# Two PSUM evacuations ahead of a low part at the quarter boundary, and the next block's normalisation ahead of the high parts on ScalarE

## The reference

```python
x = x + tanh(g_xattn) * attention(layernorm(x), ctx)    # 32 query heads, 8 key heads, dim 128
x = x + tanh(g_ffn) * ffn(layernorm(x))

def ffn(x):                                             # x is 2048 x 1024
    routing = softmax(x @ gate_w.T)                     # 8 experts
    in_scale  = routing @ in_channel_scale
    out_scale = routing @ out_channel_scale
    return (x * in_scale) @ sign(weight).T * out_scale + bias
```

## Time and profile before

| | |
|---|---|
| median of 3 runs | 1588.42 us |
| the profiled execution, its own time | 1589.38 us |
| its span, first to last instruction | 1587.6 us |
| TensorE busy (share of the span) | 1494.5 us (94%) |
| VectorE | 1034.2 us (65%) |
| GpSimd | 722.6 us (46%) |
| ScalarE | 615.2 us (39%) |
| mean granted TensorE clock, of full speed | 0.976 |

### The profile page before, as it was taken

The page is one execution under the profiler, slowest core; times in us unless marked ns, Lnnn a source line. Parts: engine busy times, 40 slices in busy tenths (PEclk is TensorE's granted clock), DMA queues, the critical chain, the costliest instruction groups (busy, mean ns, idle before and its releaser), DMA issues. The chain is left out here.

```text
span 1587.6 us, 26175 instructions
## 1 busy us (share of the span) xinstructions
PE 1494.5 (94%) x8720; PEld 1312.1 (83%) x8720; DVE 1034.2 (65%) x2375; ACT 615.2 (39%) x1183; POOL 722.6 (46%) x586
## 2 busy tenths in 40 slices
PE   6899999999999999999999399999999999769998
PEld 6778888888888888888888299999999999747776
DVE  6737878887788878887788545545545545555552
ACT  5722222322222222222222255555555555344442
POOL 6735454555546455455554333333333333135543
PEclk9999999999999999999999699999999999869999
DMA  7731122221322212222122794246954234332211
GB/s 275 270 100 54 41 79 75 73 66 40 86 66 73 66 42 83 66 73 66 53 66 66 227 398 151 74 126 202 389 189 126 79 115 124 100 146 85 95 71 62
DMA packets 90991, 184.02 MB, mean 116 GB/s; under 512 B 8976, under 2 KB 34064, under 8 KB 90768
## 3 DMA queue, kind: packets, MB, share of 16 engines
q1 hardware_dynamic: 86848, 178.95, 35.2%
q10 hardware_dynamic: 4080, 4.26, 0.8%
HBM read 129.70 MB, written 53.48 MB: 115 GB/s over the span
## 5 line engine op out<-in xcount | busy, mean ns | idle before, releaser
L51 PE MATMUL q_ps<-x_hi,w_hi 128*128 128x512 f32 x1024 | 399.5, 390 | 3.4 <-PEq L66 3.4
L53 PE MATMUL q_ps<-x_hi,w_lo 128*128 128x512 f32 x1024 | 400.9, 391 | 0.0
L52 PE MATMUL q_ps<-x_lo,w_hi 128*128 128x512 f32 x1024 | 400.0, 391 | 0.0
L913 DVE TENSOR_TENSOR vw_lo<-vw_ps,vw_hi 64x256 fp32r<-64x256 f32 x512 | 216.2, 422 | 241.0 <-ACT vw_hi L873 235.8
L902 POOL TENSOR_TENSOR w_lo<-w_raw,w_hi 128x512 fp32r<-128x512 f32 x128 | 166.1, 1299 | 297.3 <-ACT w_hi L865 297.3
L838 PE MATMUL acc_ps<-vw_hi,x_hi 128*128 128x256 f32 x1024 | 291.4, 285 | 4.9 <-DVE ahead_y L930 4.0
L839 PE MATMUL acc_ps<-vw_lo,x_hi 128*128 128x256 f32 x1024 | 290.6, 284 | 0.0
L840 PE MATMUL acc_ps<-vw_hi,x_lo 128*128 128x256 f32 x1024 | 290.5, 284 | 0.0
L873 ACT CAST vw_hi<-vw_ps 64x256 fp32r<-64x256 f32 x512 | 188.2, 368 | 177.7 <-PE vw_ps L53 172.9
L595 POOL TENSOR_TENSOR q_lo<-rot,q_hi 128x512 fp32r<-128x512 f32 x128 | 165.2, 1296 | 190.6 <-ACT q_hi L561 190.5
L51 PEld LDWEIGHTS q_ps<-x_hi,w_hi 128*128 128x128 f32 x1024 | 192.7, 188 | 45.0 <-issue 3.6
(11 more groups left out here) (132 smaller groups left out, 2448.3 us busy)
## 6 DMA issues: line engine op xcount, KB each, us to landing
w_raw<-in_wo SPq DMA_DIRECT2D x128, 256.0 KB, 2.8
w_raw<-in_wq SPq DMA_DIRECT2D x32, 512.0 KB, 5.2
probs_scratch<-pt_hi SPq DMA_DIRECT2D x64, 256.0 KB, 2.6
probs_scratch<-pt_lo SPq DMA_DIRECT2D x64, 256.0 KB, 3.2
x_hi<-probs_scratch SPq DMA_DIRECT2D x32, 512.0 KB, 8.0
x_lo<-probs_scratch SPq DMA_DIRECT2D x32, 512.0 KB, 9.6
x_in<-in_x SPq DMA_DIRECT2D x16, 512.0 KB, 4.7
ahead_y<-in_x SPq DMA_DIRECT2D x8, 1024.0 KB, 6.3
```

Of the source, the lines that this page charges most:

```text
L51: pe.matmul(out, hi, rhs_hi, start=first, stop=False, **kw)
L52: pe.matmul(out, hi, rhs_lo, start=False, stop=False, **kw)
L53: return pe.matmul(out, lo, rhs_hi, start=False, stop=last, **kw)
L913: done = nc.vector.tensor_tensor(vw_lo[at], vw_ps[i][b * SK:(b + 1) * SK, h, :], vw_hi[at].bitcast(F32), ALU.subtract)
```

## The change

Three things are done.

1. In `project`, VectorE makes the low part of the next quarter's head pair 0 as before, then evacuates banks 0 and 1, then makes the low part of head pair 1, then evacuates banks 2 and 3.
2. In `feed`, ScalarE normalises block i+1 right after the copy of the transposed routing and before the four high parts of block i.
3. GpSimd waits, once, before slot 1, for all stores of `x_q` to memory.

```diff
@@ project, VectorE, quarter @@
                 if following is not None:
-                    for hp in range(VW_AHEAD):
-                        values_low(*following, hp)
+                    values_low(*following, 0)
                 dve.wait_ge(x_q_in, 16 * (pair * NQ + q + 1))
                 for bank in range(NACC):
+                    if following is not None and bank == NACC // 2:
+                        values_low(*following, 1)
                     if bank < NACC - 1:
@@ feed, ScalarE, slot @@
                     nc.scalar.copy(r_stack_t[0:R, j, :], r_ps[0:R, 0:BT]).then_inc(r_stack_t_ready, 1)
+                if has(i, -1):
+                    normalise(i + 1, 1 - j)
+                if has(i, 0):
                     wait(act, f_done, NC * (i - 1))
                     high(i, j, 0)
                     high(i, j, 1)
@@ @@
                     high(i, j, 3)
                 some_signs(i, 7, KT)
-                if has(i, -1):
-                    normalise(i + 1, 1 - j)
                 some_signs(i + 1, 0, 3)
@@ feed, GpSimd @@
             slot(0, 0)
+            pool.wait_ge(x1_stored, 16 * B // PB * NQ)
             slot(1, 1)
```

## The result

The changed kernel took 1572.73 us, the median of 4 runs (1570.04 to 1574.38), against 1588.23 for the kernel before: ratio 0.9898, 95% interval [0.9881, 0.9915]. Measured two more times it took 1570.3 and 1570.81 us against 1588.21 and 1588.61: [0.9871, 0.9905] and [0.9875, 0.9913]. It is 15.5 to 17.9 us faster; 1571.4 was forecast. The profiled execution after has a span of 1571.5 us.

What follows compares the result with a forecast made beforehand. TensorE, busy 94% of the span, was taken as the bound. Terms -5.3 - 7.9 - 3.8 = -17.0 us took the profiled 1589.38 to 1572.4, and 0.96 lower for the median: 1571.4 us; 8-in-10 range 1568.5 to 1575.5.

Steps and rivals of the forecast that it cites:

- The three waits that the sum names: TensorE's waits: evacuation at quarter boundaries and `x1n` in steady slots gone; block 1's from 9.3 to about 5.5 us.
- Quarter boundary: `project`: 7 boundaries of 0.80 us won, 5.6 us, less 0.3 for a possible hold: -5.3 us.
- the 0.3 us for a hold at bank 2: Quarter boundary in `project`: allowance for bank 2's matmul waiting on its evacuation; bounds nothing to 1.0 us in all.
- Rival 1: Quarter boundaries: bank 2 is held after all, 3 to 5.6 us lost, 1574 to 1577 us; chance 0.09.
- Steady slots: `feed`: six waits of transposes for the normalised block go, 1.32 us each: -7.9 us, bounds 7.2 and 8.4.
- The 0.1 us by which I let the high parts slip: Steady slots, ScalarE: first high part starts at 1540.6 instead of 1540.47, behind the earlier normalisation.
- Rivals 3: Steady slots: transposes find another wait, for `xs` or late high parts; half of 7.9 lost, 1575.4 us; chance 0.05.
- 4: ScalarE in each slot: normalisation waiting for `shift` blocks the queue; slower, 1594 us at 7 us later; chance 0.02.
- 5: `feed`: `wait(act, tb_done, i)` or `f_done` could hold the normalisation's new place; no size or separate chance, others 0.01.
- Slot 0 to slot 1: `feed`: block 1's transposes start after the last `xs` part, at 1409.9 instead of 1413.74: -3.8 us.
- The reading of 2.15 us as a hold by GpSimd: Slot 0: VectorE's first low part waits for GpSimd's `x1b`; gain 3.8 us, 3.6 if the time is its own.
- Rival 2: `feed`: fast clock is back for block 1's transposes, 1.7 us less, 1569.7 us; chance 0.09.

Runs made afterwards that it cites:

- the single edit: The kernel before with only VectorE's part of the change, the new order of low parts and evacuations at the quarter boundary: 1583.74 us, ratio 0.9974.
- the two repetitions: The changed kernel measured again two more times with no edit: 1570.3 and 1570.81 us.
- the last version: Changed kernel plus x1b held back, signs and zeroing reordered, idle-time matmuls in feed's first two slots and before `project`: 1565.05 us.
- the two reorderings: On the changed kernel: GpSimd's x1b held behind block 0's low parts (alone 1570.61 us); block 0's signs, copy and zeroing reordered (alone 1569.36 us).

## Why the prediction was right

**The whole.** 1571.4 us forecast, 1572.73, 1570.3 and 1570.81 measured. By the stretches of the first profile the changed parts gave 5.7 + 3.8 + 9.2 = 18.7 us where I had 17.0; 0.8 of that is the clock behind T1 (below). The first stage was 4.6 us later in that execution and the clock 1.8 us better in the first quarter. The three waits that the sum names are gone or as short as forecast. The closeness of the single number owes something to luck.

**Quarter boundary, -5.3 forecast.** Shown: the single edit removes 2.5 + 3.2 = 5.7 us from these stretches, 0.8 for each of 7 boundaries. Mis-sized is the 0.3 us for a hold at bank 2. There is none: evacuations 1 to 3 lie about 0.1 us earlier against TensorE than I laid them (the third one starts 4.05 us behind head pair 15's first matmul, not 4.16), mainly since the first follows the bank's last matmul by 0.32 us here (1029.21 to 1029.53) and not by 0.39. So the room at bank 2 was 0.24 us. Rival 1 is excluded. The experiment with both low parts late shows that the method also gives a loss to 0.1 or 0.2 us.

**Steady slots, -7.9 forecast.** T1 to T7 is 9.24 us shorter. Five of the six slots give 1.41 us each on average, where I had 1.32 and named 1.4 as the bound. The size was off because I read one slot, and slot 6 has the shortest of the six waits (1.12 us; their mean is 1.2). Slot 6 itself gave 21.72 - 20.37 = 1.35 us: 1.29 and 0.06 more, since the 16 transposes take 1.91 us where they took 1.97. The others gave 1.38 to 1.46. The 0.1 us by which I let the high parts slip did not come. Block 1's own slot gave 2.17, of which 0.8 is the clock; in the two repetitions it gave 1.67 and 1.43. Rivals 3, 4 and 5 are excluded in the rows: no wait for `xs` or `shift` in these slots, and the order does what it says.

**Slot 0 to slot 1, -3.8 forecast.** 3.76 measured, with the wait of 5.5 us that names `xs`, and 4.1 in the two repetitions. No run separates the 0.3 us between them. The reading of 2.15 us as a hold by GpSimd, which I had argued from two rows, is shown by the experiment that moved the add.

**The clock.** Rival 2 (fast clock for block 1's transposes) came true by a fifth in one of three profiles: 3.30 us against 3.67 and 1.97, with the full clock from the first products on. In the other two they took 3.65 us, at the low clock throughout. T1 to T2 took 21.75 to 23.06 us with the low clock behind a wait of 4 to 6 us, and 20.4 where TensorE was kept busy. What I left out altogether is that the same holds for the first quarter of `project` (60.15 to 62.06 us in profiles of the changed kernel, 59.51 in the last version, with the clock back before it).

**Open.** Why the first stage ends anywhere from 87.1 to 94.6 us isn't settled. TensorE's waits for the split weights there add up to 21.7 us before, 23.0 after and 20.4 in the repetition, which explains a part. The stretch from there to `project` took between 817.0 and 818.8 us over the versions, which no edit was meant to touch; that isn't explained either. Nor was GpSimd's new wait run by itself; between `shift` and `x1b` pass 0.14 us with it (1399.73 to 1399.87) and 0.15 without.

## What to carry to other kernels

A wait that stands on an engine's queue for something else is removed by order alone: look for the gap in which that engine waits anyway, and check that the moved work fits (2.37 us of activations into a gap of 2.28 delayed nothing here, with 1.6 us of slack behind it). Size the gain from all places where the wait occurs: the one slot read had the shortest. Lay out the other engine's list by measured durations up to the next due time. For a change of 1%, compare stretches that repeat to 0.1 us rather than whole times that spread by 0.5%, and don't credit a gain in front of a stretch that may run at the low clock until the stretch behind it has been read.

## What the runs showed of the hardware

- Moving work forward into a stretch at the low clock gives part of it back: block 1's transposes came 1.4 us earlier, the low level lasted 5.6 us behind them instead of 2.9 to 4.3, and the next slot took 0.6 to 1.3 us more.
- Idle-time matmuls put into waits of up to 10 us brought block 0's and block 1's transposes to 1.9 to 2.0 us each and took, together with the two reorderings, 5.8 us off the changed kernel. A count that is right at the full clock overruns at the low one (20 matmuls: 4.63 us in one version, 6.33 in another with a granted clock of 0.72).
- A VectorE subtraction with both inputs in SBUF took 2.10 us beside GpSimd's 4.5 us add and 0.69 without it.
- The kernel before took 1584.3 to 1592.7 us over 21 runs on one chip; the normalisation alone 1576.7 to 1577.5 over 6 on the same chip.
